# Rounds of two batches in a conditional mixing and low-rank kernel: both products, both z, then the low rank of the two batches in front, with GpSimd summing z

## What is computed

```python
# x (64, 128, 2048); itok_B_0_15 (64,), itok_B_4_50 (64,)
# L0_cond_weights (16, 128, 128); L1_cond_A (64, 2048, 16); L1_cond_B (64, 16, 2048)
W = weights[itok_B_0_15]
x = x + einsum('bct,bcd->bdt', x, W)
Bx = einsum('bni,bri->bnr', x, B[itok_B_4_50])
x = x + einsum('bnr,bor->bno', Bx, A[itok_B_4_50])
```

## Time and profile before

| | |
|---|---|
| median of 3 executions | 398.72 us |
| profiled execution, its own time | 398.63 us |
| its span, first to last instruction | 396.8 us |
| mean granted TensorE clock | 0.989 of 2.4 GHz |
| TensorE matmul busy | 380.9 us, 96% |
| VectorE, ScalarE, GpSimd busy | 68%, 56%, 7% |
| moved between HBM and the core | 152.37 MB |
| share of the 16 DMA engines' span taken by packets | 96.8% |

### The profile page before, as it was taken

The page is one execution under the profiler, slowest core; times in us unless marked ns, Lnnn a source line. Parts: engine busy times, 40 slices in busy tenths (PEclk is TensorE's granted clock), DMA queues, the critical chain, the costliest instruction groups (busy, mean ns, idle before and its releaser), DMA issues.

```text
span 396.8 us, 16443 instructions
## 1 busy us (share of the span) xinstructions
PE 380.9 (96%) x6164; PEld 351.2 (89%) x6164; DVE 271.3 (68%) x576; ACT 221.5 (56%) x513; POOL 29.7 (7%) x71
## 2 busy tenths in 40 slices
PE   7899999999999999999999999999999999999970
PEld 7889999999999999999999999999999999999960
DVE  0267767766866766776776686686677677678683
ACT  2566555556555555655555655555565565565540
POOL 1200000000000000000000000000000000000000
PEclk9999999999999999999999999999999999999995
DMA  6999999999999999999999999999999999999528
GB/s 222 417 416 413 404 403 411 400 400 386 418 388 402 404 396 419 385 413 395 401 409 394 415 390 402 408 391 407 405 402 396 415 395 399 408 402 371 235 121 304
DMA packets 29103, 152.37 MB, mean 384 GB/s; under 512 B 3233, under 2 KB 3490, under 8 KB 12962
## 3 DMA queue, kind: packets, MB, share of 16 engines
q1 hardware_dynamic: 29090, 152.19, 96.8%
HBM read 85.07 MB, written 67.11 MB: 384 GB/s over the span
## 4 chain that ended last, share of the span: by engine, by line
PE 91%; DMA 3%; DVE 2%; SPq 1%; issue 1%; ACT 0%; DVEq 0%
PE f_bank L333 58%; PE low_bank L368 17%; PE z_bank L347 16%; DMA ab_in<-in_lora 2%; DVE x_out L262 1%; DVE z_pair L288 0%; DMA ids<-in_ids 0%; SPq L138 0%; DVE z_all L293 0%; SPq L125 0%; SPq L128 0%; SPq L139 0%; DVE at L280 0%; DVEq L53 0%; ACT ft L220 0%
## 5 line engine op out<-in xcount | busy, mean ns | idle before, releaser
L333 PE MATMUL f_bank<-m_sel,x_in 128*128 128x128 f32 x2048 | 246.1, 278 | 2.4 <-ACT ft L220 1.4
L333 PEld LDWEIGHTS f_bank<-m_sel,x_in 128*128 128x128 f32 x2048 | 233.6, 192 | 10.6 <-issue 1.4
L220 ACT COPY ft<-f_bank 128x512 f32<-128x512 f32 x256 | 149.6, 585 | 78.4 <-PE f_bank L333 77.5
L262 DVE TENSOR_TENSOR x_out<-low_bank,ft 128x512 f32<-128x512 f32 x252 | 156.5, 682 | 2.0
L288 DVE TENSOR_TENSOR z_pair<-z_bank,z_two 16x128 f32<-16x128 f32 x128 | 36.8, 287 | 92.8 <-ACT z_two L228 90.8
L368 PE MATMUL low_bank<-z_all,at 16*128 16x128 f32 x2016 | 75.1, 283 | 2.1 <-DVE x_out L262 2.1
L368 PEld LDWEIGHTS low_bank<-z_all,at 16*128 16x128 f32 x2016 | 62.9, 186 | 15.4 <-issue 15.4
L347 PE MATMUL z_bank<-ft,ab_in 128*16 128x128 f32 x2048 | 68.3, 274 | 0.0
L236 ACT COPY z_all<-z_all 16x128 f32<-16x128 f32 x128 | 37.8, 296 | 50.1 <-DVE z_all L293 48.6
L280 DVE STREAM_TRANSPOSE at<-ab_in 128x512 f32<-128x512 f32 x64 | 44.8, 700 | 19.1 <-DMA ab_in<-in_lora 19.1
L347 PEld LDWEIGHTS z_bank<-ft,ab_in 128*16 128x16 f32 x2048 | 50.3, 96 | 7.8 <-issue 0.2
(11 more groups left out here) (9 smaller groups left out, 2.6 us busy)
## 6 DMA issues: line engine op xcount, KB each, us to landing
x_in<-in_x SPq DMA_DIRECT2D x63, 1024.0 KB, 9.2
out<-x_out SPq DMA_DIRECT2D x62, 1024.0 KB, 7.3
ab_in<-in_lora SPq DMA_DIRECT2D x64, 256.0 KB, 8.1
out<-x_out SPq DMA_DIRECT2D x8, 256.0 KB, 4.4
w_all<-in_weights SPq DMA_DIRECT2D x1, 1024.0 KB, 7.3
x_in<-in_x SPq DMA_DIRECT2D x1, 768.0 KB, 4.6
x_in<-in_x SPq DMA_DIRECT2D x1, 256.0 KB, 3.1
w_first<-in_weights SPq DMA_DIRECT2D x2, 64.0 KB, 4.1
```

The source lines that it names most:

```text
L220: nc.scalar.copy(ft[k][u][:], f_bank[BANK_OF[u]][:]).then_inc(copied, 1)
L262: nc.vector.tensor_tensor(x_out[k][:, UNIT * u:UNIT * (u + 1)], banks_of(b)[u][:], ft[k][u][:], ALU.add).then_inc(added, 1)
L333: last = nc.tensor.matmul(f_bank[BANK_OF[u]][:, P * c:P * (c + 1)], x_in[k][:, UNIT * u + P * c:UNIT * u + P * (c + 1)], m_sel[k][:], star ...
```

## The change

Batches go in pairs, called rounds. TensorE's list for a round of batches b and b + 1 is both products, both z, then the low rank of b - 2 and of b - 1. The eight PSUM banks have no fixed use: in even rounds (kind 0) the products are in banks 5, 6, 7, in odd rounds (kind 1) in 2, 3, 4; z is in banks 0 and 1, and the low ranks take what is free (`LOW_BANKS`), in part the banks that the next round's products or z need.

The sum of z's four parts moves. ScalarE and VectorE each copy two parts of each z to SBUF (`take_z`), GpSimd does all three additions (`sum_z` of the GpSimd block), and ScalarE makes the other three copies (`place_z`). The additions read all four parts from SBUF, and there are four `z_all` instead of two. SyncE's list is written in another order. The last two batches have a list of their own: only one unit of the very last is added by VectorE, the other three have their low rank accumulated on top of the product in PSUM and are copied out by ScalarE.

The core of the diff:

```diff
 JS = UNIT // BLOCK
-BY_DVE, BY_ACT = (0, 1), (2, 3)
-BANK_OF = (0, 1, 2, 0)
-LATE = (3, 0, 1, 2)
-BODY = 4
+ROUND = 2
+BODY = 2 * ROUND
+KINDS = BODY // ROUND
+F_BANKS = ((5, 6, 7), (2, 3, 4))
+Z_BANKS = (0, 1)
+LOW_BANKS = (((2, 3, 4, 7), (0, 1, 5, 6)), ((5, 6, 7, 4), (0, 1, 2, 3)))
+LAST_F = (2, 3, 4, 2)
+LAST_LOW = (5, 6, 7, 1)
+LAST_OWN = (0, 3, 4, 2)
...
+def f_bank_of(kind, k, u, final):
+    return LAST_F[u] if final and k == ROUND - 1 else F_BANKS[kind][(UNITS * k + u) % len(F_BANKS[kind])]
...
+            def next_x(k, b):
+                sp.wait_ge(f_made, UNITS * (b - BODY + 1))
+                load_x(k, b)
+            def next_ab(k, b):
+                adapter = adapter_of(b)
+                sp.wait_ge(z_done, b - BODY + 1)
+                sp.wait_ge(a_turned, b - BODY + 1)
+                load_ab(k, adapter)
...
+                for kind in range(KINDS):
+                    k, other = ROUND * kind, ROUND * (1 - kind)
                     b = BODY * q + k
+                    if begun(b - BODY):
+                        store(k, b - BODY)
                     if not last:
-                        sp.wait_ge(f_made, UNITS * (b + 1))
-                        load_x(k, b + BODY)
-                    if begun(b - 1) and exists(k + BODY - 1, last):
-                        adapter = adapter_of(b + BODY - 1)
-                        sp.wait_ge(z_done, b)
-                        sp.wait_ge(a_turned, b)
-                        load_ab((k - 1) % BODY, adapter)
-                    if begun(b - 2):
-                        sp.wait_ge(added, UNITS * (b - 1))
-                        sp.dma_start(out[b - 2], x_out[(k - 2) % BODY][:]).then_inc(stored[(k - 2) % BODY], 16)
+                        next_x(k, b + BODY)
+                    if begun(b - BODY):
+                        store(k + 1, b + 1 - BODY)
+                    if begun(b - ROUND) and not (last and kind > 0):
+                        next_ab(other, b + ROUND)
+                        next_ab(other + 1, b + ROUND + 1)
+                    if not last:
+                        next_x(k + 1, b + 1 + BODY)
...
+            def sum_z(k, b):
+                parts = z_part[k % ROUND]
+                pool.wait_ge(z_taken_act, 2 * (b + 1))
+                pool.wait_ge(z_taken_dve, 2 * (b + 1))
+                if live(b):
+                    pool.wait_ge(z_summed, b)
+                for i in range(2):
+                    nc.gpsimd.tensor_tensor(z_pair[i][:], parts[2 * i][:], parts[2 * i + 1][:], ALU.add
+                                            ).then_inc(z_paired, 1)
+                pool.wait_ge(z_paired, 2 * (b + 1))
+                if live(b - BODY + 1):
+                    pool.wait_ge(low_done, b - BODY + 1)
+                nc.gpsimd.tensor_tensor(z_all[k][rows_of_unit(0), :], z_pair[0][:], z_pair[1][:], ALU.add
+                                        ).then_inc(z_summed, 1)
...
+                for kind in range(KINDS):
+                    k, other = ROUND * kind, ROUND * (1 - kind)
                     b = BODY * q + k
-                    if exists(k + 3, last):
-                        if live(b):
-                            pool.wait_ge(f_made, UNITS * b)
-                        pick_m((k + 3) % BODY, b + 3)
+                    if not (last and kind > 0):
+                        pick_m(other, b + ROUND)
+                        pick_m(other + 1, b + ROUND + 1)
+                    sum_z(k, b)
+                    sum_z(k + 1, b + 1)
...
+            def take_z(i, b, z_bank):
                 act.wait_ge(z_done, b + 1)
-                if live(b):
-                    act.wait_ge(z_paired, 2 * b)
-                for i in range(2):
-                    nc.scalar.copy(z_two[i][:], rows_of_z(2 * i)).then_inc(z_copied, 1)
+                if live(b - 1):
+                    act.wait_ge(z_paired, 2 * (b - 1))
+                for c in (0, 2):
+                    nc.scalar.copy(z_part[i][c][:], rows_of_z(z_bank, c)).then_inc(z_taken_act, 1)
             def place_z(k, b):
-                act.wait_ge(z_placed_dve, len(BY_DVE) * b + 1)
-                if live(b - 1):
-                    act.wait_ge(low_done, b - 1)
-                for u in BY_ACT:
-                    nc.scalar.copy(z_all[k % 2][rows_of_unit(u), :], z_all[k % 2][rows_of_unit(BY_DVE[0]), :]
-                                   ).then_inc(z_placed_act, 1)
...
+                act.wait_ge(z_summed, b + 1)
+                for u in range(1, UNITS):
+                    nc.scalar.copy(z_all[k][rows_of_unit(u), :], z_all[k][rows_of_unit(0), :]).then_inc(z_placed, 1)
...
+            def normal_round(kind, b):
+                for i in range(ROUND):
+                    copy_units(kind, i, b + i, False)
+                for i in range(ROUND):
+                    take_z(i, b + i, Z_BANKS[i])
+                for i in range(ROUND):
+                    place_z(ROUND * kind + i, b + i)
...
+            for i in range(ROUND):
+                b = BATCHES - ROUND + i
+                copy_units(1, i, b, True)
+                take_z(i, b, Z_BANKS[0])
+                place_z(ROUND + i, b)
+            act.wait_ge(stored[BODY - 1], 16 * (TURNS - 1))
+            act.wait_ge(low_done, BATCHES)
+            for u in range(1, UNITS):
+                nc.scalar.copy(x_out[BODY - 1][:, UNIT * u:UNIT * (u + 1)], bank[LAST_OWN[u]][:]).then_inc(evacuated, 1)
...
+            def take_z(i, b, z_bank):
+                dve.wait_ge(z_done, b + 1)
+                if live(b - 1):
+                    dve.wait_ge(z_paired, 2 * (b - 1))
+                for c in (1, 3):
+                    nc.vector.tensor_copy(z_part[i][c][:], rows_of_z(z_bank, c)).then_inc(z_taken_dve, 1)
...
-            def sum_tiles(k, b):
-                for i in range(2):
-                    dve.wait_ge(z_copied, 2 * b + i + 1)
-                    if i == 0 and live(b):
-                        dve.wait_ge(z_placed_dve, len(BY_DVE) * b)
-                    nc.vector.tensor_tensor(z_pair[i][:], rows_of_z(2 * i + 1), z_two[i][:], ALU.add).then_inc(z_paired, 1)
-                dve.wait_ge(z_paired, 2 * (b + 1))
-                if live(b - 1):
-                    dve.wait_ge(low_done, b - 1)
-                for u in BY_DVE:
-                    nc.vector.tensor_tensor(z_all[k % 2][rows_of_unit(u), :], z_pair[0][:], z_pair[1][:],
-                                            ALU.add).then_inc(z_placed_dve, 1)
...
+            def normal_round(kind, q):
+                b = BODY * q + ROUND * kind
+                for i in range(ROUND):
+                    take_z(i, b + i, Z_BANKS[i])
+                if begun(b - ROUND):
+                    for i in range(ROUND):
+                        add_units(ROUND * (1 - kind) + i, b - ROUND + i, q - (kind == 0), LOW_BANKS[kind][i])
+                for i in range(ROUND):
+                    turn_a(ROUND * kind + i, b + i, q + 1)
...
+            take_z(0, BATCHES - 2, Z_BANKS[0])
+            add_units(0, BATCHES - 4, TURNS - 1, LAST_LOW)
+            turn_a(BODY - 2, BATCHES - 2, TURNS)
+            turn_a(BODY - 1, BATCHES - 1, TURNS)
+            add_units(1, BATCHES - 3, TURNS - 1, LAST_LOW, (0, 1))
+            take_z(1, BATCHES - 1, Z_BANKS[0])
+            add_units(1, BATCHES - 3, TURNS - 1, LAST_LOW, (2, 3))
+            add_units(BODY - 2, BATCHES - 2, TURNS - 1, LAST_LOW)
+            add_units(BODY - 1, BATCHES - 1, TURNS - 1, LAST_OWN, (0,))
...
+                    m = UNITS * i + u
+                    if isinstance(b, int) and b == 0:
+                        pe.wait_ge(first_loaded[min(u, 2)], 16)
+                    elif u == 0:
+                        pe.wait_ge(x_loaded[k], 16 * (turns - (k == 0)))
+                    if u == 0:
+                        pe.wait_ge(m_picked, b + 1)
+                    if m >= len(F_BANKS[kind]):
+                        behind = 1 if final and i > 0 and u == 0 else 3
+                        pe.wait_ge(copied, UNITS * b + u - behind + 1)
+                    elif live(UNITS * (b - BODY) + u + 1):
+                        pe.wait_ge(added, UNITS * (b - BODY) + u + 1)
+                    to = bank[f_bank_of(kind, i, u, final)]
...
+            def sum_z(k, b, turns, z_bank, freed, taken):
                 pe.wait_ge(ab_loaded[k], 16 * turns)
                 pe.wait_ge(copied, UNITS * (b + 1))
-                if live(b):
-                    pe.wait_ge(z_paired, 2 * b)
+                if live(freed):
+                    pe.wait_ge(added, freed)
+                if live(taken):
+                    pe.wait_ge(z_taken_act, 2 * taken)
+                    pe.wait_ge(z_taken_dve, 2 * taken)
                 for u in range(UNITS):
...
+            def add_low_rank(k, b, banks, freed, taken, own=False):
                 pe.wait_ge(a_turned, b + 1)
-                pe.wait_ge(z_placed_dve, len(BY_DVE) * (b + 1))
-                pe.wait_ge(z_placed_act, len(BY_ACT) * (b + 1))
```

(44 more changed lines are left out.)

179 lines of the change are left out of this document (77 added, 102 removed).

## The result

The changed kernel takes 410.24 us (median of 4 runs, 408.01 to 412.59) against 398.72 before: a ratio of 1.0291, 95% interval 1.0258 to 1.0325. It is slower, where 390.1 us and a gain were forecast. The profiled execution is the 412.59 one; its span is 410.8 us.

A forecast was written before the change was run, and what follows sets the result against it. TensorE and the DMA engines were both taken as bounds, with transfers at 402 GB/s deciding: z of batch 60 at 359.5 plus an end of 28.8 gives a span of 388.3, time 390.1 us, range 381.5 to 399.

The forecast's parts named there:

- 11.21 us plus 0.2 of waiting for the chain: TensorE's round: 2 x 5.34 plus 0.53 for changes of kind, against 11.74 before, plus some 0.2 us waiting at the fourth unit.
- The chain: z's parts through ScalarE, GpSimd's additions, ScalarE's copies: delays the next round's first product copy; with TensorE alone 387.3 us.
- Two products in a row cost no more than one stretch, as do two z or two low ranks: TensorE's paired work: only changes of kind cost, 0.175 us each, so 0.53 a round in place of 1.06.
- the GpSimd rival: GpSimd's z additions bound the kernel; 407 us at 0.56 us each. Chances: moderate form 0.12, same time 0.05, slower 0.13.
- The first rival: Transfers give way: rate rises to 416 GB/s, adapters' slack lasts, TensorE decides; 381 to 387 us, chance 0.20.
- The adapter is what is late first: Adapter for z: 13.4 us from issue to use against 8.1 landing; the 5 us slack is used up after 10 to 16 rounds.
- 402 is, within about 1%, the rate of this mix: DMA engines: 402 GB/s taken as what they can do, so a round's 4.72 MB takes 11.74 us.
- from there every round lasts as long as its transfers: Rounds after the adapter's slack is gone: paced by transfers, 11.74 us a round at 402 GB/s.
- 359.5: Time in us when adapter 60 lands and z of batch 60 starts, set by the transfers.
- 350.5: Start in us of z of batch 60 were TensorE alone the bound, without waits: 367.5 - 15.9 - 1.1.
- The tail: From the start of z of batch 60 to the program's end: 28.8 us, half a microsecond less than before.
- I count nothing for the clock: TensorE's granted clock: stays at 1.00 despite short waits, as from 10 to 40 us before; cost nothing.

The follow-up runs named there:

- experiments 2, 3: Transfers alone, all compute left out, stores of zeros: 2 in the changed kernel's order, 3 in the order of the kernel before; 370.68 and 370.62 us.
- experiment 5: Changed kernel, all engines computing on batches 0 to 3 only, transfers running free into buffers nobody reads; 406.38 us.
- Experiment 6: Changed kernel, but every whole store leaves out the last 128 of 2048 columns, so rounds ask for 402 GB/s; 396.57 us.
- Experiment 7: Changed kernel with split adapter, x of batch 1 ahead of second w_first, first A halves behind x of batch 3; 394.64 us, 0.991 of before.
- experiment 1: Changed kernel with light transfers: x loads from batch 4 on and all stores move only 512 of 2048 columns; 390.26 us.
- 4: Changed kernel with the adapter in two loads, the half z needs asked for at the round's head; 396.99 us, ratio to before 0.9961.

## Why the prediction was wrong

**Right in the number, not in all its terms.** A round was put at 11.21 us plus 0.2 of waiting for the chain; it is 11.40. But TensorE waited for nothing longer than 0.15 us between 60 and 180 us. The chain itself came as forecast:

```profile
143.01 2.00 PE L392 MATMUL bank<-ft,ab_in 128*16 128x128 f32 x64
144.94 2.15 PE L410 MATMUL bank<-z_all,at 16*128 16x128 f32 x64
147.02 7.19 PE L376 MATMUL bank<-m_sel,x_in 128*128 128x128 f32 x62
...
206.84 1.56 ACT L264 COPY ft<-bank 128x512 f32<-128x512 f32 x3
```

(The 62 records are cut by a window's edge. The z in front of the last row starts at 200.78.) ScalarE's first copy of a round starts 5.9 to 6.1 us after the first z (6.2 was forecast) and is done 0.59 later, 0.2 to 0.3 before the fourth unit wants its bank. The 0.2 lies in the seams instead. The product stretch takes 7.34 from its start to the start of z, as its terms give. Two z in a row take 1.93 or 2.03, and two low ranks 2.08, where I had counted 1.88 and 1.99, each with one change of kind. So "Two products in a row cost no more than one stretch, as do two z or two low ranks" holds for the products alone, and that the sum came out at 11.40 is luck. GpSimd's addition was taken as 0.45 us:

```profile
L226 POOL TENSOR_TENSOR z_pair<-z_part 16x128 f32<-16x128 f32 x128 | 55.0, 446 | 232.3 <-DVE z_part L311 212.4
```

446 ns is 1.6 times VectorE's 280, not twice; the GpSimd rival (407 us by 0.56 us an addition) is refuted, though its time was the nearest to the result. The first rival had the rate right, which did rise (406 to 411 GB/s until 200 us), and the outcome wrong. The adapter is what is late first, and from about the 15th round, as forecast; the forecast had it late by a queue that grows for all parts alike, so its date is in part luck.

**The step that failed** is "402 is, within about 1%, the rate of this mix", and with it "from there every round lasts as long as its transfers". 402 was TensorE's own demand before: 4.72 MB in 11.74 us. The mix alone does 425 (experiments 2, 3), and 424 beside full compute (5). What has a limit is the one late engine. By the landings of the last part alone it carries a sixteenth of 404 to 408 GB/s in 5 and of 399 in the changed kernel from 60 to 200 us; in the old kernel it carries 402 and does not fall behind. So its limit beside this compute is some 400 GB/s, known to about 2%. The old kernel asked for 402 and could just be served, and its lag stayed bounded; the new one asks for 414. Experiment 6, which asks for 402 in the new order, stayed bounded too. So the figure was near a true limit, for a wrong reason, and the error came from what happens beyond it. I let the queue grow by 0.3 to 0.5 us a round for all parts alike and then settle at 402. In fact 15 parts follow at once and one falls behind, and once its lag has used up the adapter's slack the round goes by that one, which is then slower still: 4.72 MB in 12.61 us is 374 GB/s. It has work all the while: at every moment from 200 to 360 us at least five transfers are issued and not fully landed.

That last loss can be seen and was not explained. A packet of 8192 bytes takes 309 ns in experiment 2 (mean from 180 us on); in the changed kernel the mean is 358 ns for those started from 300 to 330 us, with 9% over 500. In 5 the mean is 310 while all queues are full and 330 to 354 after 300 us. The kernel before, whose queues are short, has 328 ns and 4% over 500 throughout. Slow packets come with short queues; why, and whether they are what slows the late engine, no run here tells.

**The sum, from 359.5 to 378.76.** From 40 to 360 us the transfers moved 125.4 MB by the stretches, 312.0 us at 402 GB/s, so 8.0 us lost. From 10 to 40 us they did 362, not 416: 4.0 us. From 360 to 378.7 at 385: 0.8. That is 12.8 of 19.3; the other 6.5 are about what the last part of the adapter that z of batch 60 waits for lands behind the 15th, 6.0 us (issued at 363.1: 15.6 against 9.6), which a common queue does not have. This split is worked out, not measured by an experiment.

**The head** was counted at nothing. By rounds of 11.40 us from 44.51 on, z of batch 60 would start at 359.7 us without any wait for an adapter; my count with the small waits, 350.5 + 27 x 0.2, is 355.9, some 3.7 earlier. By luck this is also the 359.5 of the transfers. In the head TensorE waited 1.94 us for x of batch 1, issued behind the second w_first, its granted clock was then at the 1.2 GHz level for part of the product (0.94 over 10 to 40 us; 32 records took 5.46 us, where 3.81 is usual), and it waited 1.64 us for ScalarE. Experiment 7 got back 1.3 us of it by the start of the product of batches 6 and 7.

**The tail** was mis-sized: 32.0 us from z of batch 60 in place of 28.8. 1.28 of it is z of batch 62 waiting for its adapter, and 1.45 the last two low ranks: I had them end 4.5 after z and they ended 5.95. They began 2.53 after it, not 2.1, and took 3.42 us where 64 such records usually take 2.15, at a mean granted clock of 0.57; before them TensorE had made no product for 2.53 us. "I count nothing for the clock" fails here as in the head:

```profile
387.86 1.07 PE L392 MATMUL bank<-ft,ab_in 128*16 128x128 f32 x32 [1.28 <-DMA ab_in<-in_lora]
...
398.54 3.42 PE L410 MATMUL bank<-z_all,at 16*128 16x128 f32 x64 [2.53 <-DVE x_out L318]
```

Even with the transfers hidden, head and tail, a little shorter there, put TensorE's own bound at 390.26 (experiment 1) and not 387.3.

So 410.24 is not the price of the new order of TensorE, which saves 0.34 us a round, against the 0.53 of its two changes of kind. It is that TensorE now asks for more than the slowest sixteenth carries, and that the adapter has the least slack against it. 31 rounds would have gained 0.34 us each; 15 of them lost 0.87.

**Open.** What puts 1.1 ns per recorded instruction on one DMA engine. Every execution here was recorded by the profiler, each timed one too, and I suppose that a record of each instruction is written somewhere. By an estimate, 1.1 ns at a sixteenth of 425 GB/s, 26.5, is 29 bytes an instruction. The Trainium skill ("NOTIFIC — the notification-queue block", 1. The block in one page) says that records for tracing are 16 bytes each, written to rings in memory; two of them would be 32. That would fit, but no run here was free of recording, and none shows it. If it is so, part of this slowdown belongs to the measurement, and the kernels might stand otherwise unrecorded.

## What to carry to other kernels

Look at the landing of the slowest of the 16 parts, not at the rate of all: a rate can look like a ceiling because it is the demand, and a kernel can lose to one late part while 15 are in time. When a change speeds up the engine that paces everything, first count the slack, from issue to use, of the smallest and latest-issued transfer, and ask for it at the head of the round (here 18.5 us of waits became 0.8 by moving 128 KB of each adapter). Keep loop bodies small enough that their code isn't loaded again: one-element instructions in loops of 50, 30 and 30 let the transfers end at 383 us, in loops of 350, 200 and 200 at 469.

## What the runs showed of the hardware

- In these recorded executions one of the 16 parts of each transfer falls behind by about 1.1 ns for each instruction in the trace, whatever the instruction moves (one element: 4.4 us per 100 us at 37.3 per us), while the transfers ask for more than that part carries; without compute it is 0.3 us per 100 us. With light transfers (experiment 1, 136 GB/s) nothing falls behind.
- This mix of loads and stores runs at 424 to 425 GB/s, beside full compute too (experiments 2, 3, 5), while all queues hold work; with one part behind and the others waiting for it, it did 361 (changed kernel) and 371 (experiment 5).
- A TensorE loop of 2880 instructions brought 102 code packets, 1.67 MB, and 133.0 us of waiting with no releaser in 508.2; the changed kernel's loop of 768 brought 9 in all.
- The first pass through the kernel's loop seems to cost as well: 1.91 us without a releaser at 56 us, then a product partly at the 1.2 GHz level, 9.78 us in place of 7.41 (experiment 6; in 4 it was 0.70 us, in 7 none). Code arrives at that time: the changed kernel has nine of its 13 instruction packets between 18 and 60 us. That the wait is for code was not shown.
- GpSimd's addition of two 16 x 128 tiles takes 446 ns, about as its addition of two 128 x 128 tiles (457); that of two single elements takes 184.
